# Finishing steps directly behind the tests for further tiles, and six buffers for gathered rows

## The reference, cut to what matters

```
x = x + s * g
xn = _layernorm(x, axis=-1)
s = _L1_attn_ref(xn, W_in, b_in, W_out, b_out)
g = _silu(_L1_ffn_ref(xn, router_w, gate_w, up_w, down_w))
x = x + s * g
```

## Time and profile before

| | us |
|---|---|
| median of three runs (345.4 to 347.27) | 345.54 |
| the profiled execution, as a run | 345.08 |
| its span, first to last instruction | 343.3 |
| PE busy in it | 315.3 (92%) |
| DVE, ACT, POOL busy | 228.9, 158.7, 61.5 |

### The profile page before, as it was taken

One profiled execution on the slowest core, in us unless ns is written; L12 is line 12 of the kernel. 1 busy time (PEld: TensorE's weight loads), 2 busy tenths in 40 slices (PEclk: granted clock), 3 DMA queues, 4 the chain that ended last, 5 costly groups with the idle time before them and its releaser, 6 DMA issues.

```text
span 343.3 us, 4810 instructions
## 1 busy us (share of the span) xinstructions
PE 315.3 (92%) x1602; PEld 186.8 (54%) x1602; DVE 228.9 (67%) x494; ACT 158.7 (46%) x289; POOL 61.5 (18%) x80
## 2 busy tenths in 40 slices
PE   2977989999999999999999999999989999999940
PEld 2645565454465454465545456556655676666630
DVE  3997848778475676877976763039898575446940
ACT  1476514575776655554474465523315622232310
POOL 5007750000010000000000002100503421033063
PEclk9999989999999999999999999999999999999995
DMA  7900019028091370400000006108934993038410
GB/s 250 406 6 2 0 49 201 1 61 191 1 207 45 83 169 1 124 0 3 1 1 3 0 1 207 41 2 326 361 95 118 392 428 140 30 124 258 165 53 20
DMA packets 19483, 39.19 MB, mean 114 GB/s; under 512 B 1826, under 2 KB 15363, under 8 KB 18176
## 3 DMA queue, kind: packets, MB, share of 16 engines
q1 hardware_dynamic: 17904, 35.69, 32.6%
q0 software_dynamic: 1552, 3.15, 2.6%
HBM read 34.54 MB, written 15.22 MB: 145 GB/s over the span
## 4 chain that ended last, share of the span: by engine, by line
PE 78%; DVE 15%; issue 3%; ACT 1%; DMA 1%; POOL 1%; DVEq 0%; POOLq 0%; ACTq 0%
PE ps L1728 12%; PE ps L1673 9%; PE ps L1641 8%; PE ps L1741 8%; PE ps L1663 7%; PE ps L1783 6%; PE ps L1799 6%; PE ps L1811 6%; PE ps L1546 3%; DVE nmax L1222 3%; PE ps L1580 2%; PE ps L1848 2%; PE ps L1525 2%; PE ps L1773 1%; DMA x<-in_x 1%
## 5 line engine op out<-in xcount | busy, mean ns | idle before, releaser
L1222 DVE TENSOR_REDUCE nmax<-ps 128x1 f32<-128x512 f32 x128 | 85.5, 687 | 35.0 <-PE ps L1641 34.3
L957 ACT ACTIVATE shared<-ps 128x512 f32<-128x512 f32 x128 | 74.1, 594 | 53.6 <-PE ps L1663 52.7
L1641 PE MATMUL ps<-experts 96*128 96x512 bf16 x128 | 48.2, 384 | 1.6 <-DVE experts L1229 1.1
L1663 PE MATMUL ps<-experts 99*128 99x512 bf16 x128 | 48.3, 382 | 0.0
L1741 PE MATMUL ps<-shared,experts 128*128 128x256 f32 x128 | 37.5, 386 | 0.0
L1673 PE MATMUL ps<-shared,experts 128*32 128x512 f32 x256 | 34.1, 605 | 0.3 <-ACT shared L957 0.3
L1641 PEld LDWEIGHTS ps<-experts 96*128 96x128 bf16 x128 | 12.5, 98 | 36.7 <-DVE nmax L1222 18.3
L1741 PEld LDWEIGHTS ps<-shared,experts 128*128 128x128 f32 x128 | 23.4, 190 | 8.9 <-issue 2.5
L965 ACT ACTIVATE experts<-ps 96x1024 bf16<-96x1024 bf16 x18 | 17.9, 1018 | 11.6 <-PE ps L1580 11.6
L1546 PE MATMUL ps<-late_weights,xnT 128*128 128x512 f32 (+1 forms) x64 | 22.5, 492 | 0.3 <-DVE shared L1134 0.3
L1783 PE MATMUL ps<-experts,shared 128*128 x88 | 20.9, 380 | 0.8 <-ACT shared L1032 0.8
(11 more groups left out here) (232 smaller groups left out, 516.9 us busy)
## 6 DMA issues: line engine op xcount, KB each, us to landing
experts<-in_experts SPq DMA_DIRECT2D x8, 1536.0 KB, 11.3
slot_rows<-in_empty SPq DMA_DIRECT2D x4, 2080.0 KB, 12.2
shared<-in_wgu SPq DMA_DIRECT2D x1, 2048.0 KB, 10.9
x<-in_x SPq DMA_DIRECT2D x2, 512.0 KB, 5.5
shared<-in_wdn SPq DMA_DIRECT2D x1, 1024.0 KB, 12.8
expert_results<-in_empty SPq DMA_DIRECT2D x1, 1024.0 KB, 6.9
token_rows<-x SPq DMA_DIRECT2D x1, 1024.0 KB, 16.0
token_rows<-gx SPq DMA_DIRECT2D x1, 1024.0 KB, 4.5
```

Of the source, the lines that this page charges most:

```text
L957: nc.scalar.activation(probs[:, n % 2, hh, :], ps[:, 2 + hh % 2, :], ACT.Exp, scale=float(HD) ** -0.5).then_inc(s["exp_done"], 1)
L1222: nc.vector.tensor_reduce(nmax[:, 4 * t + hh:4 * t + hh + 1], ps[:, m % 2, :], AX, ALU.max, negate=True).then_inc(s["max_done"], 1)
L1641: nc.tensor.matmul(ps[:, m % 2, :], qs[0:KS, b, GR * g + hh, P * t:P * t + P], ks[0:KS, b, g, :], start=True, stop=True).then_inc(s["score ...
L1663: nc.tensor.matmul(ps[:, 2 + hh % 2, :], ks[0:KM, b, g, P * t:P * t + P], qs[0:KM, b, GR * g + hh, :], start=True, stop=True).then_inc(s[" ...
```

## The change

Three things change. `tiles_from` is replaced by `tiles_or_drain`, whose test is turned round: the finishing steps are the body that stands directly behind the test, and the next tile is the other case. A failing test now falls through into its finishing steps, and a tile that is to run is reached by a jump over one set of them. On ScalarE the tanh of a result moves behind the next test: for tiles 6 and later it is issued two tiles on (`further_tile`), or in the finishing steps behind the copy of the hidden values (`rest`). On GpSimd there are six buffers, the two new ones in another part of the same SBUF tensor, gathers 6 to 11 are issued ahead of the scatters, and a further tile gathers only if it is number 12 or later, ahead of its own scatter. That makes four semaphores more.

```diff
--- before.py
+++ after.py
@@ -48,7 +48,7 @@
 SURE = TOK // P
 VW = 32
 EARLY = 6
-GATHERED = 4
+GATHERED = 6
 QK_AT = 8192 + 2048 + NI * S
 WGU_AT = 4096
 LN_EPS = 1e-5
@@ -472,7 +472,12 @@
         kv = Sa[:, 6144:8192].rearrange("p (j n) -> p j n", j=NT)
         rope_t = Sa[:, 4096:6144]
         yg = Sa[:, 0:2048].rearrange("p (j n) -> p j n", j=NT)
-        gathered = Sa[:, 4096:6144].rearrange("p (a n) -> p a n", a=GATHERED)
+
+        def gathered(a, lo=0, hi=2 * D):
+
+            at_ = 4096 + 2 * D * a if a < 4 else 2048 + 2 * D * (a - 4)
+            return Sa[:, at_ + lo:at_ + hi]
+
         hmT = Sa[:, 8192:9216].rearrange("p (a n) -> p a n", a=2)
         wsc = Sa[:, 3072:4096].rearrange("p (b k n) -> p b k n", b=B, k=KD)
         ysb = bin_b[:, 0:2 * D].rearrange("p (a n) -> p a n", a=2)
@@ -589,16 +594,16 @@
             dst = qs[0:KS, b, 2 * c:2 * c + 2, :] if c < 8 else ks[0:KS, b, 2 * c - 16:2 * c - 14, :]
             return src, dst
 
-        def tiles_from(eng, n_tiles, i, tile, drain):
+        def tiles_or_drain(eng, n_tiles, i, tile, drain):
 
             if i == MT:
                 drain(i)
                 return
-            with eng.If(n_tiles > i):
+            with eng.If(n_tiles < i + 1):
+                drain(i)
+            with eng.Else():
                 tile(i)
-                tiles_from(eng, n_tiles, i + 1, tile, drain)
-            with eng.Else():
-                drain(i)
+                tiles_or_drain(eng, n_tiles, i + 1, tile, drain)
 
         def place_in_stack(a, h0=0, h1=QKH):
             return stack.rearrange("p (j h) c -> p j h c", j=TB)[:, :, h0:h1, HD * a:HD * a + HD]
@@ -829,7 +834,7 @@
                     pool.wait_ge(out_store[a], 16 * n)
                 pool.wait_ge(x_sem[i % XR], 16 * (i // XR + 1))
                 nc.gpsimd.indirect_dma_start(
-                    out=gathered[:, a, :], out_offset=None, in_=xg_dram[:, :], in_offset=by_token(i),
+                    out=gathered(a), out_offset=None, in_=xg_dram[:, :], in_offset=by_token(i),
                     bounds_check=TOK - 1, oob_is_err=False).then_inc(gather_sem[a], 16)
 
             def store(i):
@@ -839,14 +844,18 @@
                 pool.wait_ge(s["out_ready"], i - EARLY + 1)
                 a = (i - EARLY) % GATHERED
                 nc.gpsimd.indirect_dma_start(
-                    out=out_rows[:, :], out_offset=by_token(i), in_=gathered[:, a, 0:D], in_offset=None, bounds_check=TOK - 1, oob_is_err=False
+                    out=out_rows[:, :], out_offset=by_token(i), in_=gathered(a, 0, D), in_offset=None, bounds_check=TOK - 1, oob_is_err=False
                 ).then_inc(out_store[a], 16)
-                if i > EARLY and i + GATHERED - 1 < MT:
-                    gather(i + GATHERED - 1)
+
+            def further_store(i):
+
+                if i >= EARLY + GATHERED:
+                    gather(i)
+                store(i)
 
             def all_stored(n):
 
-                for i in range(n, min(n + GATHERED - 1, MT)):
+                for i in range(n, EARLY + GATHERED):
                     m, a = divmod(i - EARLY, GATHERED)
                     pool.wait_ge(gather_sem[a], 16 * (m + 1))
                 for a in range(GATHERED):
@@ -866,7 +875,7 @@
             for i in range(EARLY, SURE):
                 store(i)
             n_tiles = pool.value_load(tiles_n[0:1, 0:1], min_val=SURE, max_val=MT)
-            tiles_from(pool, n_tiles, SURE, store, all_stored)
+            tiles_or_drain(pool, n_tiles, SURE, further_store, all_stored)
 
         @block.scalar
         def _(act):
@@ -1037,7 +1046,7 @@
                     act.wait_ge(s["y_ready"], k)
                 nc.scalar.activation(ytanh, ysb[:, k % 2, :], ACT.Tanh).then_inc(s["y_tanh"], 1)
 
-            def tile(i):
+            def head(i):
                 act.wait_ge(s["e_gate"], i + 1)
                 if i >= 2:
                     act.wait_ge(s["e_h"], i - 1)
@@ -1053,13 +1062,19 @@
                     key_squares(0, 0, TB)
                 if i == 1:
                     q_copy(2)
-                if i:
+                if 0 < i < SURE - 1:
                     result_tanh(i - 1)
                 if i == 1:
                     key_squares(1, 0, TB // 2)
 
+            def further_tile(i):
+
+                result_tanh(i - 2)
+                head(i)
+
             def rest(i):
                 hmT_copy(i - 1)
+                result_tanh(i - 2)
                 result_tanh(i - 1)
 
             qkv1_out(3)
@@ -1067,9 +1082,9 @@
             for n in range(KD):
                 q_copy(n)
             for i in range(SURE):
-                tile(i)
+                head(i)
             n_tiles = act.value_load(tiles_n[0:1, 0:1], min_val=SURE, max_val=MT)
-            tiles_from(act, n_tiles, SURE, tile, rest)
+            tiles_or_drain(act, n_tiles, SURE, further_tile, rest)
 
         @block.vector
         def _(dve):
@@ -1422,15 +1437,15 @@
                     nc.vector.scalar_tensor_tensor(ysb[:, k % 2, :], ytanh, 1.0, ysb[:, k % 2, :], ALU.add, ALU.mult).then_inc(s["y_ready"], 1)
                     return
                 n, a = divmod(k - EARLY, GATHERED)
-                row = gathered[:, a, :]
+                gate, row = gathered(a, D), gathered(a, 0, D)
                 dve.wait_ge(s["y_half"], k + 1)
                 dve.wait_ge(gather_sem[a], 16 * (n + 1))
-                nc.vector.tensor_tensor(row[:, D:2 * D], ysb[:, k % 2, :], row[:, D:2 * D], ALU.mult).then_inc(s["product_ready"], 1)
+                nc.vector.tensor_tensor(gate, ysb[:, k % 2, :], gate, ALU.mult).then_inc(s["product_ready"], 1)
                 dve.wait_ge(s["product_ready"], k - EARLY + 1)
                 dve.wait_ge(s["y_tanh"], k + 1)
-                nc.vector.scalar_tensor_tensor(row[:, D:2 * D], ytanh, 1.0, row[:, D:2 * D], ALU.add, ALU.mult).then_inc(s["y_ready"], 1)
+                nc.vector.scalar_tensor_tensor(gate, ytanh, 1.0, gate, ALU.add, ALU.mult).then_inc(s["y_ready"], 1)
                 dve.wait_ge(s["y_ready"], k + 1)
-                nc.vector.tensor_tensor(row[:, 0:D], row[:, D:2 * D], row[:, 0:D], ALU.add).then_inc(s["out_ready"], 1)
+                nc.vector.tensor_tensor(row, gate, row, ALU.add).then_inc(s["out_ready"], 1)
 
             def tokens(q):
 
@@ -1477,7 +1492,7 @@
                 tile(i)
                 side_work(DVE_AFTER.get(i, ()))
             n_tiles = dve.value_load(tiles_n[0:1, 0:1], min_val=SURE, max_val=MT)
-            tiles_from(dve, n_tiles, SURE, tile, lambda i: last_rows(i, TOKENS_LEFT.get(i, ())))
+            tiles_or_drain(dve, n_tiles, SURE, tile, lambda i: last_rows(i, TOKENS_LEFT.get(i, ())))
 
         @block.tensor
         def _(pe):
@@ -1871,7 +1886,7 @@
                 hidden_T(i - 1)
                 down(i - 1)
 
-            tiles_from(pe, n_tiles, SURE, tile, rest)
+            tiles_or_drain(pe, n_tiles, SURE, tile, rest)
 
 
 def kernel(**inputs):
```

## The result

| | before | after |
|---|---|---|
| runs beside each other, median (lowest to highest) | 345.2 (342.9 to 348.55), 16 runs | 341.2 (339.68 to 344.76), 16 runs |
| ratio of after to before | | 0.9891 [0.986, 0.9921] |
| profiled execution, its span | 345.08, 343.3 | 340.19, 338.3 |

Faster by 3.8 us (0.0109 of 345.2; 2.7 to 4.8 by the interval). The forecast was 340.9, so 0.3 off, and 4.6 of gain lie inside the interval. The agreement is better than the reasoning was. Part of it is luck: the forecast was counted from a median of 345.54 and the one measured here is 345.2, so the gain itself is 0.8 short. The traces show that the terms of the sum, taken together, came as forecast, and that something not foreseen took 1.2 us of them back.

A forecast was written before the change was run, and what follows sets the result against it. Bound: PE with its stop at the failing tile-11 test, then GpSimd's gathers around the last scatter. Gains of 2.1, 1.0 and 1.6 less 0.1 make 4.6, from 345.54 to 340.9 us; own range 340.0 to 342.3, wider range 339.6 to 343.2.

The forecast's parts named there:

- the sum: End of the span: 2.1 on PE, 1.0 and 1.6 for two GpSimd gathers, less 0.1, so 4.6 us less.
- The stop on PE: Before tile 10's transposes: PE's 1.90 us wait, from the failing tile-11 test's long jump over four tiles, goes.
- The three added jumps: PE, before tiles 8, 9 and 10: jumps over one set of finishing steps, 0.2 us each, covered by the sequencer's lead.
- the 0.3 that I had named as a sign: Sign on PE: all four tests of the number of tiles take under 0.3 us.
- The tail: Tile 10's transposes at 327.67, last scatter at 333.62, then 5.1 us to the span's end, 0.1 for slower scatter landing.
- The drain's nature, left open: GpSimd's 2287 ns drain at the end: own length or waiting for transfers not shown; kept whole.
- On VectorE, ScalarE and GpSimd I take it at nothing, since their long one took at most 67 ns: Added jumps before tiles 8, 9 and 10 on these three engines: no cost.
- 2.1 on PE: Last tile: 1.90 us of jump and 0.20 of transposes saved, so VectorE is done 2.10 earlier.
- 2.6 on GpSimd: Late gathers removed: 1.0 us for the one ahead of the last scatter, 1.6 for the one behind it.
- A: PE's stop stays because taken jumps disturb the fetching; the 2.1 on PE is lost: 343.0 us, chance 12%.
- C: GpSimd's scatters each wait for the landing of the one before, 2.7 us each: 344.5 us, chance 5%.
- B: Each jump before tiles 8, 9 and 10 costs PE 2.2 us, 6.6 in all: 347.5 us, chance 6%.

The follow-up runs named there:

- nest cut at 12: Kernel before with its nest of tests cut at 12 tiles in place of 15, so the failing test jumps over one tile: 344.42 us, ratio 0.9996.
- tests alone: Changed kernel with its new tests and ScalarE order, but four buffers and a gather behind each late scatter as before: 347.3 us, ratio 1.0064.
- gathers alone: Kernel before with six buffers and no gathers between the late scatters, old tests and tanh place kept: 344.71 us, ratio 0.9973.

## Why the prediction was right, and what it missed

**The stop on PE.** Gone, with no cost of the finishing steps' place. It came from the far target, as I had taken it (nest cut at 12: 367 ns), though a jump of that length is not slow each time (399 and 3136 ns for one and the same at the end). The three added jumps took 0.24 to 0.38 on PE, for 0.2, and were covered by the sequencer's lead; the first of them is over the 0.3 that I had named as a sign. The 1.90 is the measured row: 3.66 less a lead of 1.9 would be 1.8.

**The tail.** 5.95 from the transposes to the last scatter for a forecast of 5.95 (327.67 to 333.62), and 5.00 to the end of the span for 5.1. The scatter alone did land later than the gather had: GpSimd's drain starts 2.7 behind the last transfer's start, for 2.5. But the drain was shorter, 2123 ns for 2287, so that nothing of it is left in the sum. The drain's nature, left open, is settled: a length of its own.

**What failed.** It is the line "On VectorE, ScalarE and GpSimd I take it at nothing, since their long one took at most 67 ns". The test's duration was the wrong row. The price of a taken jump stands ahead of the engine's next instruction: 0.65 of "issue" where VectorE falls through, 1.14 where it jumps, and VectorE has only 0.5 to spare in tile 8. That 0.5 would have fitted into the spare time. The larger part, 1.05 to 1.24, I did not price at all: gather 6 comes late, likely because the new order brings a packet of PE's code forward onto it, and VectorE waited 0.6 for gather 6 before already. I had looked at what the new gathers would do to the transfers, which is nothing, and not at what the new code order would do to the fetching of code. Together 1.2 of the 4.6 were lost.

**What I read wrongly though the sum came out.** I added 2.1 on PE and 2.6 on GpSimd as if each could be had alone. For PE's part the runs show that it can't: the tests alone lose 0.6%, since GpSimd's row of nine transfers ends no earlier, and with PE's stop alone taken away (nest cut at 12) the aligned time falls by 0.1. The gathers alone gain 0.95 in the trace; the 2.6 of the sum stands there only if the slow product is taken off. Together they give what the sum says, less the new stop: the chain of before went over PE, and a second one, through GpSimd's row, ended within a microsecond of it.

**The rivals.** A (the stop stays) is refuted by the after trace; C too, the scatters start 1.3 to 1.5 apart and land 2.2 to 3.4 after their issue. B is true as a mechanism and does not act here.

**Open.** How much of gather 6's delay is the code packet and how much other traffic was not separated: 3.79 with the packet out of the way, 3.45 before, and 3.97 to 4.69 with a packet at about the same place, 0.7 apart. Why one and the same end jump on PE is fast in one trace and slow in another is not known beyond the time of the packets. Whether the last product of "gathers alone" runs at the lower clock in each execution is not known.

## What to carry to other kernels

Before two gains on one path are added, ask of each what the chain would be with that one alone; where two chains end within a microsecond, shortening one alone may bring nothing (0.1 here, with PE's stop alone removed). When code is reordered, price the jump on the engine with the least slack, by the idle time of the instruction behind it and not by the branch's own duration, and look at which transfer a fetch of code may fall on. At the end of a program, let an idle engine wait for the last landing, so that the last engine's drain runs beside it.

## What the runs showed of the hardware that I had not expected

- A branch taken over one set of finishing steps: 0.24 to 0.38 us in the test itself on PE; on VectorE 47 to 72 ns in the test and 0.48 (1.14 less 0.66) ahead of the next instruction. A far one on PE: 3.3 to 3.7 in the tests; the end jump over four tiles and four sets 0.31 to 0.40 in four traces and 2.9 to 3.8 in seven, the slow ones with a code packet moved during the jump.
- Where a 16 KB packet of code fell beside a 128-row gather, the gather's data were used 3.97 to 4.69 us after the issue (eight traces); where it did not, 3.45, 3.49, 3.53 and 3.79.
- GpSimd's drain takes 2.1 to 2.3 behind its last work, beside the landing of its last transfer if nothing makes it wait.
- A PE product of 2.0 us took 3.59 at a granted clock of 0.50 after a stop and a short wait, in one of the two kernels with a stop of 1.9 there; in the other the clock stayed at 1.00.
